# Attention's q and k parts stored once, stacks loaded in six transfers, expert weights loaded behind the attention rounds

## The chip, the cores and the metric

The kernel runs on one core of a Trainium2 chip. The core has a matrix engine (PE, with its weight loads shown apart as PEld), a vector engine (DVE), a scalar engine (ACT), a general engine (POOL) and a sync engine (SP), which here only issues transfers; 16 DMA engines move the data. The metric is the device time of one launch in microseconds (us), lower is better.

## The reference

Two transformer blocks with adaptive layer norm run one after the other on 16 sequences of 256 tokens and 128 features. The change lies in the attention of block 0:

```python
qkv = x @ w_qkv + b_qkv                     # 16 heads of depth 8
q, k = _rope(q), _rope(k)
scores = jnp.einsum('bhtd,bhsd->bhts', q, k) / jnp.sqrt(jnp.float32(D))
attn = jax.nn.softmax(scores, axis=-1)
out = jnp.einsum('bhts,bhsd->bhtd', attn, v)
out = jnp.transpose(out, (0, 2, 1, 3)).reshape(Bs, Ts, C) @ w_fc + b_fc
```

Behind it come a mixture of 64 experts (8 of them chosen for each token, and a shared one), the delta-rule attention of block 1, and its mixture of 8 experts.

## The kernel before, in words

Attention works in rounds, numbered n in the program and k in its Python: round n runs the projections of batch n + 2, the stack loads of batch n + 1, the first pass of scores of batch n (p1), the second pass of scores with exp and the product with v of batch n - 1 (p2), and the tail of batch n - 2. Each engine has its own instruction list, and semaphores order them; `run` calls `iteration` for rounds -3 to 17.

float32 scores are made from bfloat16: ACT cuts q and k into three parts each (`cut`, L439), all pairs of parts are stacked on 72 partitions (3 x 3 pairs x depth 8), and one matmul of 72 rows gives the score. To get the parts onto these partitions they go through DRAM. SP waits for the third cut and stores `at_part` into `qk_parts` (the tensor `bounce`), which holds all nine pairs of each batch: three stores for q (L592) and three for k (L594), each of all three parts, 192 KB. In the next round it loads the q stack (`at_qs`) and the k stack (`at_ks`) with one transfer of 72 rows of 8 KB each (L569). The q load waits for PE's first score of the round (`p1_done`) and for the stores (`part_out`); the k load waits for `nrows_in[1]`, that is for the last maxima rows of the batch before. PE waits for both (`stacked`) ahead of p1 of the next batch.

p1 (L191) gives the row maxima on DVE (L334), these are split into three parts, turned by PE (L175), copied by ACT to `at_npart`, and POOL moves them in two halves of the heads: a store to DRAM (L524, `max_parts<-at_npart`), a wait until it has landed, and a load into three more rows of the q stack (L529, `at_qs<-max_parts`). p2 (L204) waits for that load (`nrows_in[half]`): for half 0 ahead of head 0, for half 1 ahead of head 8.

The gate and up weights of the experts (`w_gu`) come in 16 pieces of 363 KB (L564). SP issues two of them at the end of each of the rounds 0 to 3 and 13 to 16, as `PIECE_ROUNDS` says; in rounds 14 to 16 SP has nothing else left but one k load. After the rounds it issues four small loads (L602), waits for the routing weights of the first chunk (`r0_kept`), stores them (L604), waits for that store and loads them spread over partitions (L609, nine transfers). Then all engines meet at the end of the block, and the experts' block starts, whose PE and ACT wait for all of `ffn0_loaded`: the 16 pieces and the four small loads.

Of the kernel before, what the change touches and what calls it, by code (L numbers as in the profile page):

```python
# [14 lines left out]
BF16 = mybir.dt.bfloat16  # L15
# [7 lines left out]
BATCH, SEQ = 16, 256  # L23
TOK = BATCH * SEQ
TILES = TOK // P
HEADS, DEPTH = 16, 8
# [9 lines left out]
PARTS = 3  # L36
PAIRS = PARTS * PARTS
ROWS = PAIRS * DEPTH
# [4 lines left out]
BUFS = 3  # L43
PEELED = 4
FIRST = -3
STACK_DMAS = 2
OUT_DMAS = 2 * PARTS
VW = 32
PIECE_ROUNDS = (0, 1, 2, 3, 13, 14, 15, 16)


def attention(nc, T, A, x_fm, x_tm, mod):
# [11 lines left out]
    with ExitStack() as ctx:  # L64
        def sb(name, shape, dt=F32):
            return ctx.enter_context(nc.sbuf_tensor(name, shape, dt))

        def sem(name):
            return ctx.enter_context(nc.semaphore(name))
# [6 lines left out]
        part = sb("at_part", [P, PARTS, 2 * SEQ], BF16)  # L76
# [21 lines left out]
        r0_bufs = (r0_sfc[:], r0_w[:], r0_hi[:], r0_lo[:], r0_th[:], r0_tl[:], r0_gs[:], r0_picked[:], r0_sig[:], r0_top[:],  # L98
                   r0_den[:], r0_rden[:])
        r0_ln = LayerNorm(nc, ctx, "r0_ln", T, r0_xc, T["h_fm"][:, 0:CHUNK], r0_nt, 0, 1)  # L100
        bounce = nc.dram_tensor("qk_parts", [BUFS, 2, PARTS, PARTS, DEPTH, HEADS, SEQ], BF16, kind="Internal").ap()
        nbounce = nc.dram_tensor("max_parts", [BUFS, 2, PARTS, HALF, SEQ], BF16, kind="Internal").ap()
        ps = T["psum"]
        P1, P2, OB, M0, M1 = [0, 1], [2, 3], (4, 5), 6, 7
# [17 lines left out]
        part_out = sem("at_part_out")  # L122
        stacked = sem("at_stacked")
# [6 lines left out]
        nrows_in = [sem(f"at_nrows_in{i}") for i in range(2)]  # L130
# [19 lines left out]
        def live(k):  # L150
            return {
                "xn": 0 <= k + 3 < BATCH, "proj": 0 <= k + 2 < BATCH, "load": 0 <= k + 1 < BATCH, "p1": 0 <= k < BATCH,
                "p2": 0 <= k - 1 < BATCH, "tail": 0 <= k - 2 < BATCH,
            }
# [5 lines left out]
        def run(eng, iteration):  # L160
            for n in range(FIRST, PEELED):
                iteration(n, n)
            with eng.Fori(0, (BATCH - 3 - PEELED) // BUFS) as i:
                for k in range(PEELED, PEELED + BUFS):
                    iteration(BUFS * i + k, k)
            for n in range(BATCH - 3, BATCH + 2):
                iteration(n, n)

        @block.tensor
        def _(pe):  # L170
# [8 lines left out]
            def scores(n, k, g, part=None):  # L179

                f = live(k)
                for h in heads(g, part):
                    if f["p1"]:
                        if h == 0:

                            pe.wait_ge(stacked, 16 * STACK_DMAS * (n + 1))
                        if k > 0 or h >= 2:
# [232 lines left out]
        def _(act):  # L420
# [10 lines left out]
            def cut(n, k, i):  # L431

                if i == 0:
                    act.wait_ge(qk_ready, n + 3)
                    if k >= -1:
                        act.wait_ge(part_out, 16 * OUT_DMAS * (n + 2))
                else:
# [112 lines left out]
        @block.sync  # L550
        def _(sp):
            def held(name, x):

                if isinstance(x, int):
                    return x
                r = sp.alloc_register(name)
                sp.reg_mov(r, x)
                return sp.snap(r)

            def load_weights(piece):  # L560

                start, name = (WG, "wg") if piece < WEIGHT_PIECES else (WU, "wu")
                at, size = piece % WEIGHT_PIECES, HIDDEN_ALL // WEIGHT_PIECES
                sp.dma_start(T["w_gu"][:, start + at * size:start + (at + 1) * size], A[name][:, at * size:(at + 1) * size])\  # L564
                    .then_inc(T["ffn0_loaded"], 16)

            def load_stack(buf, stack, q):

                sp.dma_start(stack[0:ROWS, buf, :, :], bounce[buf, q].rearrange("b a d h t -> (b a d) h t")).then_inc(stacked, 16)  # L569

            def iteration(n, k):
                f = live(k)
                cut = held(f"cut_{k}", PARTS * (n + 3))
                seen = held(f"seen_{k}", HEADS * n + 1)
                out = held(f"out_{k}", 16 * OUT_DMAS * (n + 2))
                rows_in = held(f"rows_in_{k}", 16 * n)
                if f["load"]:
                    if f["p1"]:

                        sp.wait_ge(p1_done, seen)  # L580
                    sp.wait_ge(part_out, out)
                    load_stack((k + 1) % BUFS, qs, 0)
                    if f["p2"]:

                        sp.wait_ge(nrows_in[1], rows_in)
                    load_stack((k + 1) % BUFS, ks, 1)
                if f["proj"]:

                    sp.wait_ge(part_ready, cut)
                    buf = (k + 2) % BUFS  # L590
                    for i in range(PARTS):
                        sp.dma_start(bounce[buf, 0, i].rearrange("a d h t -> (d h) a t"), part[:, :, 0:SEQ]).then_inc(part_out, 16)  # L592
                    for i in range(PARTS):
                        sp.dma_start(bounce[buf, 1, :, i].rearrange("b d h t -> (d h) b t"), part[:, :, SEQ:2 * SEQ])\  # L594
                            .then_inc(part_out, 16)
                if k in PIECE_ROUNDS:
                    for i in range(2):
                        load_weights(2 * PIECE_ROUNDS.index(k) + i)

            run(sp, iteration)  # L600
            for name in EARLY_LOADS:
                sp.dma_start(T[name][:], A[name]).then_inc(T["ffn0_loaded"], 16)  # L602
            sp.wait_ge(r0_kept, 1)
            sp.dma_start(T["rw_dram"][:, 0:CHUNK], r0_fm).then_inc(r0_out, 16)  # L604
            sp.wait_ge(r0_out, 16)
            rb = T["rw"][:, 1, :].bitcast(F32).rearrange("p (s c) -> p s c", c=CHUNK)
            for j in range(RB_SLOTS):
                for first, last, e in owners(j):
                    sp.dma_start(rb[first:last, j, :], T["rw_dram"][e:e + 1, 0:CHUNK].broadcast_to([last - first, CHUNK]))\  # L609
                        .then_inc(T["rb_in"][j], 16)  # L610
# [355 lines left out]
WEIGHT_PIECES = 8  # L966
# [24 lines left out]
def owners(j):  # L991

    rows = range(P * j, P * (j + 1))
    return [(max(HIDDEN * e, rows[0]) - rows[0], min(HIDDEN * (e + 1), rows[-1] + 1) - rows[0], e)
            for e in range(rows[0] // HIDDEN, rows[-1] // HIDDEN + 1)]
# [1038 lines left out]
def adaln_two_blocks(nc, *args):  # L2034
    A, out = dict(zip(NAMES, args[:-1])), args[-1]
    with ExitStack() as ctx:
# [23 lines left out]
        with ExitStack() as first:  # L2060
            for name, shape in dict(mean=[P, TILES], rstd=[P, TILES], w_qk=[P, 2 * D], w_v=[P, D], w_fc=[P, D],
                                    at_v=[P, BUFS, 2, HEADS, VW]).items():
                sb(name, shape, scope=first)
            sb("at_ks", [P, BUFS, HEADS, SEQ], BF16, scope=first)
            T["rw_dram"] = nc.dram_tensor("rw_fm", [EXPERTS, TOK], F32, kind="Internal").ap()
            setup(nc, T, A)
            attention(nc, T, A, T["x_fm"], T["x_tm"],
                      (T["scale1"][:, 0, :], T["shift"][:, 0, :], T["gate"][:, 0, :], T["ga_bfc"][:, :]))
# [62 lines left out]
```

## Time and profile before

| | us |
|---|---|
| median of 3 runs (lowest, highest) | 1827.18 (1826.78, 1829.08) |
| profiled execution, its own time | 1828.58 |
| span of the profile, first to last instruction | 1826.5 |

Times in the rows are us from the span's start. The attention rounds lie between about 20 and 377, the experts' block begins at 391.6. A timeline row has the start, the time taken, engine, line, operation, tiles, shapes and count, and in brackets how long the engine had been idle and what ended that. A windows row has the busy time of each engine in the stretch with its count of instructions, then the granted TensorE clock as a share of full speed, the mean busy share of the 16 DMA engines and what they moved.

### The profile page before, as it was taken

The page shows a single profiled execution, that of the slowest core. Times are in us where ns is not written, and L with a number is a line of the kernel's source. Part 1 is how long each engine was busy: PE and PEld are TensorE (multiplying, and loading weights), DVE is VectorE, ACT ScalarE, POOL GpSimd, SP SyncE. Part 2 cuts the span into 40 slices and gives each one's busy share as a digit, 9 for nine tenths or more (in the row PEclk, how much of TensorE's full clock was granted, in tenths as well). Part 3 has the DMA queues.
Part 4 walks back from the last instruction along what each step waited for, and adds up shares of the span by engine and source line. Part 5 has one row for each costly group of instructions (what it writes and reads, how often), then busy time and mean ns, then how long its engine had stood idle before and what let it go on. Part 6 is the DMA issues. An engine that isn't in the chain of part 4 may idle for free.

```text
span 1826.5 us, 25499 instructions
## 1 busy us (share of the span) xinstructions
PE 1659.0 (91%) x7212; PEld 1027.0 (56%) x7212; DVE 1366.2 (75%) x2636; ACT 819.6 (45%) x1533; POOL 691.8 (38%) x628
## 2 busy tenths in 40 slices
PE   3888888869989999999999999999998899899999
PEld 2455555446655656556665565655655555555555
DVE  4777777656979988979969889799698587544444
ACT  1566767657644234243352342533525543433333
POOL 2011111100002945928739469187394475000000
PEclk9989989989999999999999999999999999999999
DMA  6554445246575877677767666666671111111110
GB/s 199 152 157 129 119 111 152 89 125 215 180 207 188 222 205 204 210 209 214 215 189 203 187 188 197 189 197 204 190 194 52 41 47 52 35 57 53 52 52 23
DMA packets 172698, 269.49 MB, mean 148 GB/s; under 512 B 23748, under 2 KB 61981, under 8 KB 170053
## 3 DMA queue, kind: packets, MB, share of 16 engines
q1 hardware_dynamic: 168691, 266.33, 49.9%
q10 hardware_dynamic: 1874, 1.36, 0.2%
q0 software_dynamic: 2048, 0.79, 0.2%
q8 instruction: 37, 0.61, 0.1%
q14 instruction: 48, 0.39, 0.1%
HBM read 233.78 MB, written 34.62 MB: 147 GB/s over the span
## 4 chain that ended last, share of the span: by engine, by line
PE 36%; DVE 16%; issue 10%; POOL 10%; ACT 3%; DMA 3%; SPq 1%; DVEq 0%; POOLq 0%; ACTq 0%
PE psum L1528 10%; PE psum L1368 6%; POOL e_prod L1986 6%; PE psum L1370 6%; PE psum L1369 6%; PE psum L1383 5%; DVE psum L1897 4%; POOL e_phi L1986 3%; DVE e_hm L1900 2%; DVE e_vbar L1755 2%; DVE e_y L1755 1%; DVE e_state L1850 1%; DMA e_ring<-w_split 1%; PE psum L1462 1%; DMA rw<-rw_fm 1%
## 5 line engine op out<-in xcount | busy, mean ns | idle before, releaser
L1694 ACT ACTIVATE e_gu<-psum 128x512 f32<-128x512 f32 (+1 forms) x368 | 219.3, 598 | 545.5 <-PE psum L1370 284.3
L1368 PE MATMUL psum<-e_hhi,e_ring 128*128 128x512 f32 x704 | 434.0, 616 | 19.7 <-DMA e_ring<-w_split 11.5
L1383 PE MATMUL psum<-e_hm,w_d 128*128 128x512 f32 (+1 forms) x736 | 382.6, 601 | 15.0 <-DVE e_hm L1903 7.2
L1986 POOL TENSOR_TENSOR e_prod<-e_state,e_phi 128x512 f32<-128x512 f32 x256 | 353.4, 1417 | 2.4 <-POOL e_phi L1986 1.7
L1897 DVE TENSOR_TENSOR psum<-psum,rw 128x512 f32<-128x512 f32 x352 | 243.4, 692 | 90.9 <-PE psum L1370 85.1
L1935 DVE TENSOR_TENSOR e_hm<-psum,rw 128x512 f32<-128x512 f32 x256 | 174.6, 688 | 178.0 <-ACT psum L1722 176.9
L1369 PE MATMUL psum<-e_hhi,e_ring 128*128 128x512 f32 x704 | 279.0, 396 | 0.0
L1370 PE MATMUL psum<-e_hlo,e_ring 128*128 128x512 f32 x704 | 278.8, 396 | 0.0
L1900 DVE TENSOR_TENSOR e_hm<-psum,e_gu 128x512 f32<-128x512 f32 x352 | 243.5, 692 | 39.4 <-ACT e_gu L1694 15.7
L1528 PE MATMUL psum<-e_hm,w_gu 128*128 128x512 f32 x512 | 262.9, 598 | 6.6 <-DVE w_d L1916 5.5
L1722 ACT ACTIVATE psum<-psum 128x512 f32<-128x512 f32 x256 | 148.8, 582 | 254.7 <-PE psum L1370 238.8
L334 DVE TENSOR_REDUCE at_negm<-psum 128x2 f32<-128x512 f32 x256 | 163.0, 684 | 68.7 <-PE psum L191 67.8
L1368 PEld LDWEIGHTS psum<-e_hhi,e_ring 128*128 128x128 f32 x704 | 133.2, 189 | 139.7 <-issue 92.4
L1369 PEld LDWEIGHTS psum<-e_hhi,e_ring 128*128 128x128 f32 x704 | 133.4, 190 | 95.6 <-issue 82.6
L1383 PEld LDWEIGHTS psum<-e_hm,w_d 128*128 128x128 f32 (+1 forms) x736 | 136.0, 189 | 65.2 <-DVE e_hm L1900 18.7
L1986 POOL TENSOR_TENSOR e_prod<-e_vbar,e_phi 128x512 f32<-128x512 f32 x128 | 169.7, 1357 | 2.5
L1368 PE MATMUL psum<-e_hhi,w_gu_r 128*128 128x512 f32 x208 | 156.4, 752 | 10.1 <-DVE e_hlo L1741 8.1
L428 ACT ACTIVATE at_p<-psum 128x512 f32<-128x512 f32 x256 | 142.1, 590 | 26.2 <-PE psum L204 23.7
L1370 PEld LDWEIGHTS psum<-e_hlo,e_ring 128*128 128x128 f32 x704 | 132.6, 188 | 31.6
L1986 POOL TENSOR_TENSOR e_phi<-e_prod 128x480 f32<-128x480 f32 x32 | 30.6, 988 | 273.2 <-ACT e_beta L1653 273.2
L204 PE MATMUL psum<-at_qs,at_ks 75*128 75x256 bf16 x512 | 105.2, 290 | 14.2 <-DMA at_qs<-max_parts 12.3
L191 PE MATMUL psum<-at_ks,at_qs 72*128 72x256 bf16 x512 | 110.3, 302 | 8.2 <-DVE at_negm L334 3.5
(304 smaller groups left out, 2181.0 us busy)
## 6 DMA issues: line engine op xcount, KB each, us to landing
e_ring<-w_split SPq DMA_DIRECT2D x308, 256.0 KB, 4.2
rw<-rw_fm SPq DMA_DIRECT2D x192, 176.0 KB
qk_parts<-at_part SPq DMA_DIRECT2D x96, 192.0 KB, 3.1
rw<-gates_fm SPq DMA_DIRECT2D x72, 256.0 KB, 3.2
w_split<-e_ring SPq DMA_DIRECT2D x44, 256.0 KB, 2.7
rw<-rw_fm SPq DMA_DIRECT2D x64, 160.0 KB
at_qs<-qk_parts SPq DMA_DIRECT2D x16, 576.0 KB
at_ks<-qk_parts SPq DMA_DIRECT2D x16, 576.0 KB
```

The lines of the kernel that those rows point to most:

```text
L334: nc.vector.tensor_reduce(negm[:, k % BUFS, h // HALF, h % HALF, :], ps[:, P1[h % 2], :].rearrange("p (t s) -> p t s", t=2), AX.X, ALU.max ...
L1368: pe.matmul(out, w_hi, x_hi, start=first, stop=False)
L1369: pe.matmul(out, w_lo, x_hi, start=False, stop=False)
L1370: return pe.matmul(out, w_hi, x_lo, start=False, stop=last)
L1383: mm = pe.matmul(ps[:, ACC, :], weights_at(T, WD + P * j, P)[0:rows(j), :], hm[0:rows(j), slot(j), :], start=(j == 0), stop=(j == HT - 1))
L1528: pe.matmul(ps[:, ACC, :], weights_at(T, w2_low(j), P), hm[:, j % RING1, :], start=(j == 0), stop=(j == T1 - 1))\
L1694: a(act_g[0:r, j % 2, :], ps[0:r, GB[j % 2], :], ACT.Silu).then_inc(silu_done, 1)
L1722: a(ps[:, GU1[j % 2], :], ps[:, HB[j % 2], :], ACT.Gelu).then_inc(gelu_done, 1)
L1897: v.tensor_tensor(ps[:, bank(j), :], ps[:, bank(j), :], rb[:, s, :], ALU.mult).then_inc(gu_done, 1)
L1900: v.tensor_tensor(hm[:, slot(j), :], ps[:, bank(j), :], act_g[:, j % 2, :], ALU.mult).then_inc(hm_done, 1)
L1935: v.tensor_tensor(hm[:, j % RING1, :], ps[:, GU1[j % 2], :], rb[:, e % RB_SLOTS, :], ALU.mult).then_inc(m_done, 1)
L1986: ins = tt(out[:, at], x[:, at], y[:, at], op)
```

## The change

Each part is stored once: `qk_parts` has one copy of the three parts for q and one for k, and SP stores them with two transfers instead of six. The stacks are built by the loads: three transfers of 24 rows for q, each of all three parts, and three for k, each of which repeats one part three times by a source with step 0. The expert weights leave the rounds: behind the last round SP waits for both halves of the last maxima rows, and then issues all 16 pieces, ahead of the four small loads.

```diff
-STACK_DMAS = 2
-OUT_DMAS = 2 * PARTS
+STACK_DMAS = 2 * PARTS
+OUT_DMAS = 2
 VW = 32
-PIECE_ROUNDS = (0, 1, 2, 3, 13, 14, 15, 16)
...
-        bounce = nc.dram_tensor("qk_parts", [BUFS, 2, PARTS, PARTS, DEPTH, HEADS, SEQ], BF16, kind="Internal").ap()
+        bounce = nc.dram_tensor("qk_parts", [BUFS, 2, PARTS, DEPTH, HEADS, SEQ], BF16, kind="Internal").ap()
...
             def load_stack(buf, stack, q):
 
-                sp.dma_start(stack[0:ROWS, buf, :, :], bounce[buf, q].rearrange("b a d h t -> (b a d) h t")).then_inc(stacked, 16)
+                for b in range(PARTS):
+                    if q == 0:
+                        src = bounce[buf, 0].rearrange("a d h t -> (a d) h t")
+                    else:
+                        src = bounce[buf, 1, b].unsqueeze(0).broadcast_to([PARTS, DEPTH, HEADS, SEQ])
+                    sp.dma_start(stack[b * PARTS * DEPTH:(b + 1) * PARTS * DEPTH, buf, :, :], src).then_inc(stacked, 16)
...
-                    for i in range(PARTS):
-                        sp.dma_start(bounce[buf, 0, i].rearrange("a d h t -> (d h) a t"), part[:, :, 0:SEQ]).then_inc(part_out, 16)
-                    for i in range(PARTS):
-                        sp.dma_start(bounce[buf, 1, :, i].rearrange("b d h t -> (d h) b t"), part[:, :, SEQ:2 * SEQ])\
+                    for q in range(2):
+                        sp.dma_start(bounce[buf, q].rearrange("a d h t -> (d h) a t"), part[:, :, q * SEQ:(q + 1) * SEQ])\
                             .then_inc(part_out, 16)
-                if k in PIECE_ROUNDS:
-                    for i in range(2):
-                        load_weights(2 * PIECE_ROUNDS.index(k) + i)
 
             run(sp, iteration)
+            for half in range(2):
+                sp.wait_ge(nrows_in[half], 16 * BATCH)
+            for piece in range(WEIGHT_PIECES):
+                load_weights(piece)
+                load_weights(WEIGHT_PIECES + piece)
             for name in EARLY_LOADS:
                 sp.dma_start(T[name][:], A[name]).then_inc(T["ffn0_loaded"], 16)
             sp.wait_ge(r0_kept, 1)
```

## Rows read from the trace of the kernel before

**Rows 1.** Windows view: three attention rounds, then the slow-clock stretch of the third.

```profile
core 0: us, PE busy (x) PEld busy (x) DVE busy (x) ACT busy (x) POOL busy (x), PEclk, DMA share, GB/s
143.90:162.50 18.60, 16.34 (x156) 10.36 (x155) 15.26 (x35) 13.55 (x27) 2.79 (x5) 1.00 0.46 132
181.30:202.00 20.70, 17.99 (x156) 10.83 (x155) 15.72 (x35) 13.41 (x27) 2.86 (x5) 0.92 0.43 117
339.40:361.40 22.00, 17.11 (x146) 10.59 (x147) 11.73 (x26) 11.49 (x21) 3.79 (x7) 0.84 0.11 35
...
341.70:348.50 6.80, 5.27 (x33) 3.49 (x34) 1.04 (x2) 2.67 (x5) 0.53 (x1) 0.50 0.03 6
```

**Rows 2.** Waits of PE from 42 to 376: us in total, times, longest.

```profile
PE psum L204 <- DMA at_qs<-max_parts: 12.3, 6, 4.9
...
PE psum L191 <- DMA at_ks<-qk_parts: 1.9, 1, 1.9
```

**Rows 3.** Timeline of PE at the two longest of these waits.

```profile
62.68 0.61 PE L204 MATMUL psum<-at_qs,at_ks 75*128 75x256 bf16 x2 [4.85 <-DMA at_qs<-max_parts]
...
337.94 0.38 PE L191 MATMUL psum<-at_ks,at_qs 72*128 72x256 bf16 x2
343.23 0.61 PE L204 MATMUL psum<-at_qs,at_ks 75*128 75x256 bf16 x2 [4.90 <-DMA at_qs<-max_parts]
```

**Rows 4.** Timelines of POOL and SP ahead of them, and one undisturbed move (150.85).

```profile
53.02 0.71 POOL L524 DMA_DIRECT2D max_parts<-at_npart  x1 [38.81 <-ACT at_npart L487]
...
54.95 1.53 SPq L564 DMA_DIRECT2D w_gu<-in_wg  x2
...
56.62 0.51 POOL L529 DMA_DIRECT2D at_qs<-max_parts  x1 [2.90 <-DMA max_parts<-at_npart]
...
150.85 0.50 POOL L529 DMA_DIRECT2D at_qs<-max_parts  x1 [1.70 <-DMA max_parts<-at_npart]
...
330.44 0.32 SPq L569 DMA_DIRECT2D at_ks<-qk_parts  x1
330.80 3.70 SPq L564 DMA_DIRECT2D w_gu<-in_wu  x6
...
339.34 0.50 POOL L529 DMA_DIRECT2D at_qs<-max_parts  x1 [6.01 <-DMA max_parts<-at_npart]
```

**Rows 5.** Timelines of SP and PE: first stores, first stack loads, first scores.

```profile
28.61 1.49 SPq L592 DMA_DIRECT2D qk_parts<-at_part  x3
...
34.15 0.38 SPq L569 DMA_DIRECT2D at_qs<-qk_parts  x1
...
42.09 1.04 PE L191 MATMUL psum<-at_ks,at_qs 72*128 72x256 bf16 x4 [1.88 <-DMA at_ks<-qk_parts]
```

**Rows 6.** Windows view: a k stack load by itself, then weight pieces by themselves.

```profile
153.80:155.90 2.10, 0.92 (x8) 0.49 (x7) 2.07 (x5) 1.60 (x3) 0.00 (x0) 1.00 0.80 199
...
336.00:339.00 3.00, 2.33 (x24) 1.09 (x22) 2.61 (x8) 1.67 (x3) 0.00 (x0) 1.00 1.04 401
```

**Rows 7.** Timelines of SP, POOL and PE in one middle round.

```profile
152.90 0.30 SPq L569 DMA_DIRECT2D at_ks<-qk_parts  x1
154.96 1.48 SPq L592 DMA_DIRECT2D qk_parts<-at_part  x3
...
161.33 0.50 POOL L529 DMA_DIRECT2D at_qs<-max_parts  x1 [3.47 <-DMA max_parts<-at_npart]
...
162.78 0.38 PE L191 MATMUL psum<-at_ks,at_qs 72*128 72x256 bf16 x2
163.95 0.39 PE L204 MATMUL psum<-at_qs,at_ks 75*128 75x256 bf16 x2 [0.79 <-DMA at_qs<-max_parts]
```

**Rows 8.** Timelines of PE and SP from the last maxima rows to the block's end.

```profile
368.99 0.61 PE L204 MATMUL psum<-at_qs,at_ks 75*128 75x256 bf16 x4
...
385.28 0.51 SPq L604 DMA_DIRECT2D rw_fm<-r_xc  x1
387.62 3.44 SPq L609 DMA_DIRECT2D rw<-rw_fm  x9
```

## The prediction, made before the changed kernel ran

> **What bounds the kernel now.** The page comes first: the profiled execution took 1828.58 us with a span of 1826.5, and the diff touches only the part up to 391 us, so nothing behind the experts' start is worked on here; that part shifts as a whole. Then the windows view round by round, to see what a round costs and whether the DMA engines are its limit. They are not: a round takes 18.6 us at full clock and 20.7 when part of it runs at the lower clock, PE is busy for 16 to 18 of these and DVE for 15, while the DMA engines are less than half busy [rows 1]. So traffic that is removed gives time only where PE waits for a transfer, and the waits of PE are the next view. Over the attention stage PE waits 12.3 us for the maxima rows and 1.9 us for a stack [rows 2]; the rest of its gaps end with DVE or ACT. The timeline then shows where: two waits, of 4.85 and 4.90 us, are 9.75 of the 12.3, one in round 1 and one in round 15 [rows 3]. In both POOL's small moves were under way together with weight pieces. A move that lands undisturbed releases POOL 1.7 us after its issue, but the two moves of those places took 2.90 and then some 6 us (56.62 to PE's start at 62.68), and 6.01 and then 3.9 us [rows 3, 4]. SP had issued two pieces at 54.95 and six from 330.80 on. That is what the change can win; all else must be looked at for what it costs.
>
> **The stores.** Six stores of 192 KB become two. Three take SP 1.49 us to issue [rows 5], so issue falls from 3 us to 1 us a round. In the middle rounds nobody waits for them directly: SP's next q load waits for PE's first score, later than they land. Their traffic does delay POOL's half 0 move: 3.47 us instead of 1.70, with the stores issued from 154.96 on and the second move issued at 161.33 [rows 4, 7]. PE paid for that with 0.79 us at 163.95 [rows 7]; all such waits together are 12.3 - 9.75 = 2.5 us, of which I count at most 1.5 in the twelve middle rounds. Before the first round the stores are on the path: issued from 28.61 on, and SP starts the loads at 34.15 [rows 5]. Two fewer us of issue and a third of the bytes make that about 2.5 us earlier, 31.6.
>
> **The stack loads.** The bytes stay the same, 0.59 MB for each stack. Two transfers become six; at the 0.30 us that one load takes to issue [rows 7] SP spends some 1.3 us more a round, in stretches in which it waits anyway. The open price is the k load. Its three transfers read a source whose outermost count is 3, with step 0, which no large transfer of the trace has. Fast end: it runs as the load of 72 rows does, which by itself moved 199 GB/s with a DMA share of 0.80 [rows 6]; with about 0.9 us from issue to the first byte (152.90 to 153.80) and 0.5 at the end that lands in 4.5 us. Slow end: the three copies go to three of the sixteen engines. The weight pieces move 401 GB/s with all of them busy, 25 GB/s for each [rows 6]; three then give 75 GB/s, 7.9 us for 0.59 MB, and 9.3 us from issue to landing. I take the slow end: the same rows show that the spread follows a transfer's shape (128 rows keep all engines busy, 72 rows only 0.80 of them), and the shape has 3 outermost now.
>
> The Trainium skill, page "DMA: Bandwidth & Descriptors", section "Why a DMA increments its semaphore by 16 and not by 1", says that a transfer uses the largest number up to 16 which divides the outermost counts of both its sides. By that rule 72 rows would take 12 engines, 0.75 of them, and the trace has 0.80; 24 rows against 3 copies would take 3. Its section "Rules for kernel authors" warns of just this form, a leading broadcast of few copies. No row here shows three engines at work.
>
> What does 9.3 us hit? In the middle rounds the time from the k load's issue to PE's next first scores is 9.9 us in a round at full clock (152.90 to 162.78, [rows 7]), and some 2 us more in the longer rounds [rows 1], about half of the twelve; so the load just makes it, and each us beyond 9.9 costs a us in the six short ones, beyond 12 in all. The two new stores come behind the load on its three engines and land at about 11 us after its issue, when SP and ACT are just about to ask for them. POOL's half 0 move also falls into this time: it loses the stores' traffic and gets the k load's, on three engines only. Together I take +0.6 us for the middle rounds, between -1.5 (the waits above gone) and +6 (half a us in each).
>
> **Start.** At the slow end the loads start at 31.6, the q stack takes some 4 us and the k stack 7.9 us on the engines that both use, and first scores come at about 43.6 instead of 42.09 [rows 5]: 1.5 us late. POOL's first move, at 53.02, shifts by that to 54.5; without weights the two moves take about 2.5 us (1.7 and the issue itself) and 2.6 (161.33 to 163.95 is a second move without weights up to PE's start, [rows 4, 7]), so p2 starts at 59.6 instead of 62.68: a gain of 3.0 us, and not the full 4.85.
>
> **Round 15.** The k load of the last batch is issued at 330.44 and PE's scores start at 337.94, 7.5 us later [rows 3, 4]. At 9.3 us these scores start at 339.7, 1.8 us late, and p2 follows at about 340.7, if POOL's moves have landed by then (its first one was issued by 333.3, 6.01 us ahead of 339.34; an answer after 1.7 us and 2.6 from there give 337.6, and up to 3 more beside the k load). Against 343.23 that is a gain of 2.5 us. Behind the old wait the clock was 0.50 for 6.8 us [rows 1], where a middle round with a share of 0.92 over 20.7 us has about 3.3. Half speed over the 3.5 us in excess costs at most 1.7 us; I take half of it, 0.8.
>
> **The weights at the end.** SP wakes when the last rows land, at 368.99, where PE starts its p2 on them [rows 8]. 16 pieces are 5.9 MB, 14.8 us at 401 GB/s [rows 6]; six pieces took 3.70 us to issue [rows 4], so issue (9.9 us) is hidden by the data. With 0.9 us ahead of the first byte and some 1.5 us for the four small loads all is in at about 386.2. The store of the routing weights is issued at 385.28 and was answered 2.34 us later, at 387.62 [rows 8]; its data now queues behind the last pieces, a loss of 0.5 us. What hides the rest is attention's tail and the routing from 369 to 385, which uses no transfer. The slowest rate of the rows, the stack load's 199 GB/s [rows 6], is the other bound: 6.2 MB would then take 31 us and end at 401, a loss of 15 us. The rate of the same transfers is the nearer row.
>
> **Sum.** -3.0 (start) - 2.5 (round 15) - 0.8 (clock) + 0.6 (middle rounds) + 0.5 (end) = -5.2 us. From 1828.58 that is 1823.4 for the profiled execution. It stands 1.4 us above the median of the runs; from 1827.18 the forecast is 1822.0.
>
> **Rivals.** *The k load is as wide as before.* Then it lands in 4.5 us, first scores come at about 39, and POOL's moves put p2 at 54.7: a gain of 8.0 us. Round 15 gains the whole 4.9, the clock 0.8 and the middle rounds 1.5, less 0.5 at the end: -14.7, 1812.5. For it: the bytes and the 8 KB rows are those of the load that ran at 199 GB/s. Against it: the outer count of 3. Chance 0.22.
>
> *The weights at the end eat the gain.* At 290 GB/s the 6.2 MB end at 391.3, the loss is 5.5 us and the sum about 0: 1827. At 330 GB/s the time would be 1825, at 245 GB/s 1831, and at the bound of 199 GB/s 1836. For it: all is in one queue, and the routing store stands behind it. Against it: the 401 GB/s were measured on the same transfers, and nothing else runs. Chance 0.15.
>
> *The k load is late in every round.* If three engines move less than 75 GB/s, or POOL's rows and the stores stretch their queue, it lands 12 us after its issue, say: PE then waits 2.1 us in the six short rounds and 2.7 us more than forecast in round 15, 15 us less the 0.6 of the sum, so 1836. At 13 us all twelve rounds wait and it is 1850. The sign turns at about 10.7 us of landing, 64 GB/s. For it: the load has no margin in the short rounds. Against it: three engines have fewer rivals for memory and ports than twelve. Chance 0.17.
>
> **How the numbers follow.** The forecast has 0.46. A measurement of this kernel tells about 0.2%, 3.7 us, from no change. The forecast itself lies between 1815 and 1828 (the start from -8 to -1, middle rounds from -1.5 to +6), 0.40 of it faster and 0.06 the same. With the wide load's 0.22, faster has 0.62; the late weights give 0.12 to the same and 0.03 to slower; the late k load gives 0.16 to slower and 0.01 to the same: 0.19 and 0.19. The range is 1811 to 1835: it takes in the wide load, most of the late weights and the mildest late k loads, and leaves out the rest of these.
>
> **What would show it.** Right: PE's waits for the maxima rows in rounds 1 and 15 fall below 1 us; the windows around a k load show a DMA share near 0.2 and some 75 GB/s; PE waits for `at_ks` in round 15 and a little in tight middle rounds; the routing store is answered within 3 us of its issue. Wrong: a k load at 0.7 to 0.8 share (the wide rival); PE waiting for `at_ks` in every round; the block's end more than 2 us later after the last maxima rows than the 18.6 us from 368.99 to 387.62; or the clock, if the rounds' lower stretches change in number, which I can't forecast and which are worth some 1.7 us each.

## The result, and the profile after

The changed kernel takes 1836.91 us (median of 7 runs, 1833.38 to 1846.11) against 1827.18 (7 runs, 1820.63 to 1832.50): the ratio, which goes by all runs and not by the medians, is 1.0065, with a 95% interval of 1.0037 to 1.0093. It is slower, by 7 to 17 us, where 1822.0 was forecast. Its profiled execution took 1833.38 us with a span of 1831.4, which is the fastest of its runs. The accounting below therefore covers 4.9 us of the difference, less than the lower end of that interval.

PE's timeline after, at the places of [rows 3, 5 and 8] and at the start of round 14's first scores (328.77; before it was 320.92):

```profile
43.49 1.03 PE L190 MATMUL psum<-at_ks,at_qs 72*128 72x256 bf16 x4 [5.38 <-DMA at_ks<-qk_parts]
...
62.75 0.61 PE L203 MATMUL psum<-at_qs,at_ks 75*128 75x256 bf16 x2 [3.94 <-DMA at_qs<-max_parts]
...
328.77 0.38 PE L190 MATMUL psum<-at_ks,at_qs 72*128 72x256 bf16 x2
...
349.09 0.39 PE L203 MATMUL psum<-at_qs,at_ks 75*128 75x256 bf16 x2
...
372.79 0.61 PE L203 MATMUL psum<-at_qs,at_ks 75*128 75x256 bf16 x4
```

SP's timeline after, with the first stores and loads, a middle round, and the end:

```profile
28.62 0.92 SPq L596 DMA_DIRECT2D qk_parts<-at_part  x2
31.41 1.13 SPq L573 DMA_DIRECT2D at_qs<-qk_parts  x3
32.59 2.33 SPq L573 DMA_DIRECT2D at_ks<-qk_parts  x3
...
153.64 2.19 SPq L573 DMA_DIRECT2D at_ks<-qk_parts  x3
155.87 0.96 SPq L596 DMA_DIRECT2D qk_parts<-at_part  x2
...
372.13 0.37 SPq L563 DMA_DIRECT2D w_gu<-in_wg  x1
...
389.08 0.53 SPq L608 DMA_DIRECT2D rw_fm<-r_xc  x1
392.77 3.44 SPq L613 DMA_DIRECT2D rw<-rw_fm  x9
396.79 0.36 SPq L1315 DMA_DIRECT2D w_d<-in_wd  x1
```

With the same points of before these rows give the time stage by stage (the first `w_d` load of the experts was issued at 391.64 before):

| up to | before | after | of this stage | forecast |
|---|---|---|---|---|
| p2 of batch 0 | 62.68 | 62.75 | +0.07 | -3.0 |
| first scores of batch 14 | 320.92 | 328.77 | +7.78 | +0.6 |
| p2 of batch 14 | 343.23 | 349.09 | -1.99 | -2.5 |
| p2 on the last rows | 368.99 | 372.79 | -2.06 | -0.8 |
| routing store issued | 385.28 | 389.08 | 0.00 | 0 |
| routing loads issued | 387.62 | 392.77 | +1.35 | +0.5 |
| first `w_d` load of the experts | 391.64 | 396.79 | 0.00 | 0 |

The sum is +5.15, and 0.25 comes back in the experts. So the end of the attention stage went nearly as forecast, and the loss lies in the start, which gained nothing, and in the middle rounds. POOL's timeline after shows what happens at both places (the first move of batch 0, half 0 and half 1 of a middle round, then half 0 of batch 14):

```profile
53.99 0.71 POOL L523 DMA_DIRECT2D max_parts<-at_npart  x1 [39.78 <-ACT at_npart L486]
58.73 0.51 POOL L528 DMA_DIRECT2D at_qs<-max_parts  x1 [4.03 <-DMA max_parts<-at_npart]
...
151.63 0.50 POOL L528 DMA_DIRECT2D at_qs<-max_parts  x1 [2.10 <-DMA max_parts<-at_npart]
157.81 0.54 POOL L523 DMA_DIRECT2D max_parts<-at_npart  x1 [5.67 <-ACT at_npart L486]
164.40 0.51 POOL L528 DMA_DIRECT2D at_qs<-max_parts  x1 [6.05 <-DMA max_parts<-at_npart]
...
341.60 0.54 POOL L523 DMA_DIRECT2D max_parts<-at_npart  x1 [4.54 <-ACT at_npart L486]
346.65 0.50 POOL L528 DMA_DIRECT2D at_qs<-max_parts  x1 [4.51 <-DMA max_parts<-at_npart]
```

A move is two transfers, a store and a load; the number in brackets at the load is the time that POOL was idle until the store was answered. The half 0 move of the same batch was answered after 3.47 us before [rows 7]; now it takes 6.05, and over the twelve middle rounds (batches 2 to 13) 4.45 to 6.05, against 2.6 to 4.35 before. The half 1 move, whose load goes out 6 us before half 0's store, is nearly as quick as it was (1.65 to 2.3 us, but 4.3 for batch 13, where it was 3.4). What is in flight beside half 0 is the k load of 153.64, with the stores of 155.87 behind it. The windows of that stretch, of a round, and of the routing store after:

```profile
core 0: us, PE busy (x) PEld busy (x) DVE busy (x) ACT busy (x) POOL busy (x), PEclk, DMA share, GB/s
124.22:144.66 20.44, 17.99 (x155) 10.87 (x154) 15.82 (x36) 13.44 (x26) 2.78 (x5) 0.92 0.28 80
...
160.00:163.00 3.00, 3.00 (x17) 1.86 (x19) 2.51 (x4) 1.99 (x4) 0.00 (x0) 0.50 0.20 64
...
389.00:393.00 4.00, 0.00 (x0) 0.00 (x0) 0.00 (x0) 0.06 (x1) 0.00 (x0) 0.50 0.46 126
```

From 160 to 163 only the tail of the k load and POOL's small packets are under way: a share of 0.20 and 64 GB/s, where a k load by itself had 0.80 and 199 [rows 6]. A whole round moves 80 GB/s instead of some 120 to 130 [rows 1], and is no shorter. PE's waits for transfers over the attention stage after:

```profile
PE psum L203 <- DMA at_qs<-max_parts: 11.3, 10, 3.9
...
PE psum L190 <- DMA at_ks<-qk_parts: 7.0, 2, 5.4
```

Before, the wait for the rows was 12.3 us in 6 times, nearly all in two places [rows 2]; now it is 11.3 in 10 times. From 80 to 320 us it rose from 1.5 to 5.9 us. The two waits for the k stack are at 43.49 (5.38) and at 82.05 (1.63).

Waits are not the whole of the middle rounds. Their windows, from p2 of batch 0 to the first scores of batch 14, before and then after:

```profile
core 0: us, PE busy (x) PEld busy (x) DVE busy (x) ACT busy (x) POOL busy (x), PEclk, DMA share, GB/s
62.68:320.92 258.24, 231.50 (x1966) 140.28 (x1967) 195.64 (x432) 172.75 (x332) 34.99 (x63) 0.93 0.47 131
...
62.75:328.77 266.02, 235.74 (x1967) 141.05 (x1968) 196.19 (x433) 173.60 (x332) 35.05 (x63) 0.90 0.27 78
```

For the same matmuls PE is busy 4.2 us longer, at a granted clock of 0.90 instead of 0.93. These are means; single stretches show 1.00 or 0.50, and the mean says how much of each there was.

### The profile page after: what moved, and what is told of

Same layout as the page of the kernel before. It is cut to its first block, busy times and chain, and to the rows that moved or that the text cites. A ratio compares the mean times of both kernels' runs of the same rounds, so it can differ in the third digit from the quotient of the medians.

```text
span 1831.4 us, 25497 instructions
## 1 busy us (share of the span) xinstructions
PE 1664.1 (91%) x7212; PEld 1027.3 (56%) x7212; DVE 1366.3 (75%) x2636; ACT 820.4 (45%) x1533; POOL 692.0 (38%) x628
## 4 chain that ended last, share of the span: by engine, by line
PE 32%; DVE 20%; issue 11%; POOL 7%; DMA 3%; ACT 3%; SPq 1%; DVEq 1%; POOLq 0%; ACTq 0%
PE psum L1532 10%; PE psum L1372 5%; PE psum L1374 5%; PE psum L1373 5%; DVE psum L1901 5%; POOL e_prod L1990 4%; PE psum L1387 4%; POOL e_phi L1990 3%; DVE e_hm L1904 3%; DMA e_ring<-w_split 2%; DVE e_vbar L1759 2%; DVE e_state L1854 2%; DVE e_y L1759 2%; PE psum L1466 1%; DVE e_hm L1939 1%
## 5 line engine op out<-in xcount | busy, mean ns | idle before, releaser
L203 PE MATMUL psum<-at_qs,at_ks 75*128 75x256 bf16 x512 | 106.4, 293 | 13.3 <-DMA at_qs<-max_parts 11.3
```

## The experiments

Each ratio is against runs of before on the same chip; "waits" are PE's for the maxima rows and for the k stack up to 420 us. Theory N: what costs is POOL's half 0 move, answered only behind the narrow k load. Rivals: W, the weights at the end; T, the number of transfers; later L, PE's own k stack lands late; B, bytes alone.

**e1_weights_only.** Before, with the weight pieces moved behind the rounds and nothing else:

```diff
-PIECE_ROUNDS = (0, 1, 2, 3, 13, 14, 15, 16)
...
             run(sp, iteration)
+            for half in range(2):
+                sp.wait_ge(nrows_in[half], 16 * BATCH)
+            for piece in range(WEIGHT_PIECES):
+                load_weights(piece)
+                load_weights(WEIGHT_PIECES + piece)
```

> Only the weights move behind the rounds; stores and stacks stay as before. Theory N (the narrow k load on three engines is what costs, through POOL's half 0 move): the two long waits of PE go, -8 to -10 us, the end gives back 1.4, the rounds in the middle stay; about 1819, 6 to 9 us below before. Theory W (the weights at the end are what costs): 2 us or more above before, as in the changed kernel.

1819.13 us, ratio 0.9933 (0.9908 to 0.9958), waits 4.2 and 1.8 us; the routing store was answered after 3.97 us (370.79 to 374.76). Moving the weights is a gain of some 12 us in spite of the store; W falls.

**e2_stacks_only.** The changed kernel with the weight pieces back in their rounds.

```diff
+PIECE_ROUNDS = (0, 1, 2, 3, 13, 14, 15, 16)
```

> Only the stores and stack loads change; the weights stay in their rounds. Theory N: as slow as the changed kernel or slower, 1836 to 1846, POOL's half 0 move answered some 6 us after its issue in the middle rounds. Theory W: no slower than before, 1822 to 1828.

1859.3 us, ratio 1.0155 (1.0125 to 1.0184). PE's waits:

```profile
PE psum L204 <- DMA at_qs<-max_parts: 30.3, 15, 6.1
...
PE psum L191 <- DMA at_ks<-qk_parts: 17.2, 6, 6.1
```

So the new stores and loads are the loss, and a larger one than I expected: with the pieces in the rounds too, PE waits 30.3 us for the rows and 17.2 for the k stack itself. Added up, e1's -0.67% and e2's +1.55% make +0.9%, which the intervals just allow beside the measured +0.65%.

**e3_depth_outer.** The changed kernel with the rows of both stacks in another order, so that the k load's source has 8 outermost and not 3 (the q load's 8 and not 24); the count of transfers and the bytes stay.

```diff
-                        src = bounce[buf, 0].rearrange("a d h t -> (a d) h t")
+                        src = bounce[buf, 0].rearrange("a d h t -> d a h t")
...
-                        src = bounce[buf, 1, b].unsqueeze(0).broadcast_to([PARTS, DEPTH, HEADS, SEQ])
+                        src = bounce[buf, 1, b].unsqueeze(1).broadcast_to([DEPTH, PARTS, HEADS, SEQ])
```

> The changed kernel with the rows of each stack in another order, depth outside and part inside, so that each transfer's source has 8 outermost instead of 3 (k) or 24 (q); same bytes, same six loads and two stores, same products. Theory N: the k load moves 170 GB/s or more and lands in 5 us, POOL's half 0 move is answered in 2.0 to 2.6 us, PE waits under 2 us in all for the maxima rows, 1811 to 1818. Theory T (six loads instead of two are what costs, by their number on SP and in the queues): no faster than the changed kernel, 1834 to 1840.

1819.87 us, ratio 0.9936 (0.991 to 0.9961), waits 9.3 us (13 times, longest 2.0) and 3.3. The shape of the transfers alone is worth some 1.3%, and T falls. But N had the way wrong here. The waits did not go below 2 us as expected: from 80 to 320 us PE waits 8.7 us for the rows, more than the 5.9 of the changed kernel. Half 0 moves of the middle rounds were answered in 2.2 to 5.1 us, and half 1 moves were slower than there (3.00 and 3.19 us at 147.13 and 166.91), perhaps beside the q load, which has 8 outermost now too; that was not tried. What e3 gains lies mostly in the start, where p2 of batch 0 begins at 56.53 instead of 62.75, and in the middle rounds, 258.9 us instead of 266.0, where PE is busy 230.4 us instead of 235.7 at a clock of 0.95 instead of 0.90.

**e4_k_as_before.** The changed kernel with k stored three times and loaded by one transfer of 72 rows, as before; q keeps its one store and three loads.

```diff
+        kbounce = nc.dram_tensor("k_parts", [BUFS, PARTS, PARTS, DEPTH, HEADS, SEQ], BF16, kind="Internal").ap()
...
+                if q == 1:
+                    sp.dma_start(stack[0:ROWS, buf, :, :], kbounce[buf].rearrange("b a d h t -> (b a d) h t")).then_inc(stacked, 16)
+                    return
...
+                    for i in range(PARTS):
+                        sp.dma_start(kbounce[buf, :, i].rearrange("b d h t -> (d h) b t"), part[:, :, SEQ:2 * SEQ])\
+                            .then_inc(part_out, 16)
```

> The changed kernel with the k side as before: parts of k stored three times, one load of 72 rows; the q side stays changed (one store, three loads of 24 rows). Theory N: the narrow load is gone, POOL's half 0 move is answered in 2.5 to 3.3 us beside four stores, 1813 to 1821. Theory T: four loads instead of six leave half of the loss, 1830 to 1834.

1815.64 us, ratio 0.9929 (0.9902 to 0.9957): faster than both kernels. PE's waits:

```profile
PE psum L204 <- DMA at_qs<-max_parts: 3.3, 4, 1.5
...
PE psum L191 <- DMA at_ks<-k_parts: 2.6, 1, 2.6
```

The k side alone is the loss, and with e3 its load's form. From 80 to 320 us PE waits 1.2 us for the rows, and the half 0 moves are answered after 2.9 us in the mean, against 4.9 in the changed kernel. Against e1 the q side brings nothing that these intervals can tell.

**e5_spare_narrow and e6_spare_wide.** These leave e4's k load as it is and add idle traffic behind it, 590 KB a round that no instruction reads, in the narrow form or in the wide one. Only SP waits for it, a round later and once behind the rounds.

```diff
                     load_stack((k + 1) % BUFS, ks, 1)
+                    if k >= 0:
+                        sp.wait_ge(r0_out, spare_in)
+                    buf = (k + 1) % BUFS
+                    spare = [ks[96:120, 0, :, :], ks[96:120, 1, :, :], qs[96:120, 0, :, :]]
+                    for b in range(PARTS):
+                        src = bounce[buf, 0, b].unsqueeze(0).broadcast_to([PARTS, DEPTH, HEADS, SEQ])  # e5
+                        src = bounce[buf, 0].rearrange("a d h t -> (a d) h t")  # e6
+                        sp.dma_start(spare[b], src).then_inc(r0_out, 16)
```

> This is e4 (k stored three times and loaded by one transfer of 72 rows, q changed, weights behind the rounds; 1815.6 us) with 590 KB a round of idle traffic behind the k load: three transfers of one q part repeated three times, 24 rows each, in the same form as the changed kernel's k load, into rows of the stacks' tiles that no instruction reads, so that neither the matmuls nor the k load depend on them. Theory N (the narrow load costs because POOL's move of the half 0 maxima is answered only behind it): the move's answer goes from about 2 to 5 us and more in every round, TensorE waits 9 to 14 us in all for the move, and the time is 1830 to 1840 us, most of the way back to the changed kernel's 1837. Rival L (the narrow load costs because TensorE's own k stack lands late, and the move is a bystander): the k load is as wide and early as in e4, so 1814 to 1822 us, waits as in e4 (3.3 and 2.6 us).

> e4 with the same 590 KB of idle traffic a round at the same place, but as three transfers of 24 different rows, in the form of the q loads. Theory N: the traffic is spread over more engines, each holds the move for 2 us at most, TensorE waits 4 to 7 us in all for the move, 1815 to 1823 us. Rival B (bytes cost, whatever engines carry them: stores, loads and moves share the memory): the same as e5, within 3 us.

e5 took 1880.6 us, ratio 1.0284 (1.0258 to 1.0311); e6 1849.84 us, ratio 1.0124 (1.009 to 1.0158). Against e4's ratio that is 3.6% and 2.0%. PE's waits, of e5:

```profile
PE psum L204 <- DMA at_qs<-max_parts: 46.6, 14, 5.1
...
PE psum L191 <- DMA at_ks<-k_parts: 2.7, 1, 2.7
```

and of e6:

```profile
PE psum L204 <- DMA at_qs<-max_parts: 30.1, 15, 5.4
...
PE psum L191 <- DMA at_ks<-k_parts: 3.0, 1, 3.0
```

L falls as the only cause: PE's k stack is as early as in e4, 2.7 us of waits, and the time is lost all the same, in the wait for the moves. But both sizes are far outside what N expected, and the answer to the move's store does not tell e5 from e6: in the middle rounds it took 4.65 to 5.2 us in e5 and 4.5 to 6.9 in e6. Traffic on more engines holds it too, if there is this much of it. What differs is the move's second transfer. From its load to PE's start on the rows, one round of e5 and then one of e6:

```profile
181.47 0.51 POOL L529 DMA_DIRECT2D at_qs<-max_parts  x1 [4.78 <-DMA max_parts<-at_npart]
186.24 0.61 PE L204 MATMUL psum<-at_qs,at_ks 75*128 75x256 bf16 x2 [2.79 <-DMA at_qs<-max_parts]
...
173.81 0.50 POOL L529 DMA_DIRECT2D at_qs<-max_parts  x1 [6.11 <-DMA max_parts<-at_npart]
175.89 0.39 PE L204 MATMUL psum<-at_qs,at_ks 75*128 75x256 bf16 x2 [1.45 <-DMA at_qs<-max_parts]
```

That is 3.1 to 4.8 us in the middle rounds of e5 in which PE waited, and 2.0 to 2.2 in e6 from batch 3 on. The other half of the difference is PE's clock: over the middle rounds e5 took 301.8 us and e6 272.9, and of these 28.9 us PE was busy for 14.6, at a granted clock of 0.86 instead of 0.91. So form and bytes both count, and in the same bytes the narrow form cost nearly twice as much, where both transfers of the move were held and PE spent longer at the lower clock. N holds for the way in which the narrow load reaches the move; it was too narrow in its condition and left out the clock.

**e7_store_by_act and e8_half_earlier.** Two tries at the end of e4: the routing store on ScalarE's own queue, and half of the weight pieces ahead of the last half 1 move.

```diff
+            act.wait_ge(r0_kept, 1)
+            nc.scalar.dma_start(T["rw_dram"][:, 0:CHUNK], r0_fm).then_inc(r0_out, 16)
```

```diff
             for half in range(2):
                 sp.wait_ge(nrows_in[half], 16 * BATCH)
-            for piece in range(WEIGHT_PIECES):
-                load_weights(piece)
-                load_weights(WEIGHT_PIECES + piece)
+                for piece in range(WEIGHT_PIECES // 2 * half, WEIGHT_PIECES // 2 * (half + 1)):
+                    load_weights(piece)
+                    load_weights(WEIGHT_PIECES + piece)
```

> e4 with one change at the end: the routing weights' first store is issued by ScalarE on its own queue and not by SyncE behind the 16 weight pieces. If the 1.3 us that the routing store took more in the changed kernel comes from its place behind the weight pieces in SyncE's queue, its answer comes within 2.5 us (it took 3.7 to 4.0) and the time falls by 1 to 1.6 us against e4: 1814 us. If it comes from the 410 GB/s that the pieces still move, the answer takes 3.5 to 4 us and the time is e4's, 1815.6 us.

> e4 with the first eight of the 16 weight pieces issued already behind the last half 0 move and before the half 1 move, some 8 us earlier. The routing store then meets the tail of the small loads only and is answered within 2.5 to 3 us (gain 0.7 to 1.5 us); the last half 1 move shares the engines with eight pieces of data and lands 1 to 5 us later, of which the cover in front of it hides some. Sum: 1813 to 1820 us, no more than 0.2% from e4.

e7: 1820.95 us, ratio 0.9956 (0.9936 to 0.9976); e8: 1822.17 us, ratio 0.9965 (0.9943 to 0.9987). Neither beats e4. In e7 the store still took 3.98 us (372.10 to 376.08), so it is not its place in SP's queue. The windows of e7 show the last of the weights still moving up to it, and beside it:

```profile
368.00:372.00 4.00, 1.73 (x8) 0.86 (x8) 2.53 (x14) 1.56 (x3) 0.73 (x1) 1.00 1.03 406
372.00:376.00 4.00, 0.00 (x0) 0.00 (x0) 0.00 (x0) 0.07 (x1) 0.00 (x0) 0.66 0.54 163
```

In e8, where the weights had landed, it took 2.33 us (381.51 to 383.84), as before; but the last half 1 move went out 24.7 us behind the last batch's first scores (336.29 to 360.96) instead of 21.1 in e4 (334.73 to 355.86), which costs more.

**e9_k_spread and e10_k_early.** The changed kernel with two of the three k transfers, or all of them, issued right behind the q loads, ahead of SP's wait for the half 1 rows.

```diff
+                    load_stack((k + 1) % BUFS, ks, 1, range(2))             # e10: all three
                     if f["p2"]:
 
                         sp.wait_ge(nrows_in[1], rows_in)
-                    load_stack((k + 1) % BUFS, ks, 1)
+                    load_stack((k + 1) % BUFS, ks, 1, range(2, PARTS))      # e10: none
```

> The changed kernel with the same nine transfers a round in the same forms, only issued elsewhere: two of the three k transfers go out right behind the q loads (in the profile after 146.2 us instead of 153.6), the third stays where all three stood. Theory N says that what costs is the small move that falls into the narrow load: two transfers are done some 6 us after issue, before the half 0 move of 157.8 us; the third needs 3 us and is done at 157. Half 0 is answered in 1.5 to 3 us again (6.05 in the changed kernel), the half 1 move (149.0 and 151.6) meets the tail of the early pair and takes some 1 to 2 us more, and the time comes to 1816 to 1826 us. Rival B (the bytes and the narrow form cost wherever they stand): no more than 3 us from the changed kernel's 1837.

> The same, with all three k transfers right behind the q loads, 7.5 us earlier than in the changed kernel: the narrow load then covers 146 to 156 us, where the half 1 move stands and not the half 0 move. Theory N: half 0 is answered in 1.5 to 3 us, half 1 in 4 to 6 us (2.1 in the changed kernel), TensorE's wait for at_qs moves to heads 8 and up, and the k stack is never waited for; 1820 to 1840 us by how much cover half 1 has. Rival L (the k stack's late landing): the waits for the k stack go from 7.0 us to at most 2.6 and with them the time, to 1825 to 1831, whichever move stands in the load.

e9 took 1862.14 us, ratio 1.0186 (1.016 to 1.0212), with waits of 35.6 and 6.3 us; e10 took 1899.81 us, ratio 1.039 (1.0362 to 1.0418), with 58.0 and 5.8. POOL's timeline in a middle round of e10, half 0, half 1 and half 0 again:

```profile
184.99 0.50 POOL L528 DMA_DIRECT2D at_qs<-max_parts  x1 [1.64 <-DMA max_parts<-at_npart]
...
201.97 0.50 POOL L528 DMA_DIRECT2D at_qs<-max_parts  x1 [4.96 <-DMA max_parts<-at_npart]
...
211.90 0.50 POOL L528 DMA_DIRECT2D at_qs<-max_parts  x1 [1.65 <-DMA max_parts<-at_npart]
```

This is the cleanest sign of the mechanism: the delay moved with the load. Half 0 fell to 1.64 us, its undisturbed time [rows 4], and half 1 rose from 2.10 to 4.96. The packet records of the traces say the same in more detail. Each store of a move ends in 16 packets of 4 bytes. In the middle rounds of the changed kernel 13 of half 0's 16 had ended 2.0 us after its issue, and the last three 4.0 to 5.7 us after it, in every one of the twelve rounds; half 1's were all early but for batch 13. In e10 it is half 1 that has three late ones, 4.2 us or more after its issue, in all twelve. In e9 both were held: in one round half 1 for 5.06 us and half 0 for 3.76, about as long as beside the stores before (3.47, [rows 7]).

The times I expected were wrong, and the rows give three reasons. PE's start behind the e10 move above:

```profile
196.48 0.53 POOL L523 DMA_DIRECT2D max_parts<-at_npart  x1 [3.07 <-ACT at_npart L459]
...
205.95 0.61 PE L203 MATMUL psum<-at_qs,at_ks 75*128 75x256 bf16 x2 [4.46 <-DMA at_qs<-max_parts]
```

First, less work covers half 1: PE is ready for it some 5 us after its store (205.95 less 4.46 is 201.49; 4.7 to 5.4 us in e9 and e10), and ready for half 0 only 6.0 to 7.4 us after its store in those rounds of the changed kernel, behind the start, in which it waited. In e9 the whole half 1 move, from store to PE's start, took 7.3 to 8.2 us, no longer than half 0 in the changed kernel (7.1 to 8.2), and it cost 2.2 to 3.1 us in each round with a wait, instead of 0.2 to 2.0. Second, in e10 the load was held as well, 4.0 us from 201.97 to 205.95 where 2.1 is usual. Third, PE was busy longer for the same matmuls: 265.8 us over the middle rounds of e10, at a granted clock of 0.81, and 247.2 in e9, at 0.86. Behind SP's wait for the half 1 rows the k load stands at the less bad of the two places.

## Why the prediction was wrong, point by point

**The k load's form: right.** Three engines, forecast at 75 GB/s and a share near 0.2; 64 GB/s and 0.20 were measured in the window of its tail. The Trainium skill's rule (page "DMA: Bandwidth & Descriptors", section "Why a DMA increments its semaphore by 16 and not by 1") gave three engines of sixteen, 0.19, and the trace agrees with 0.20. The landing was a little mis-sized: by the packet records the load's last packet ended 9.95 to 10.3 us after its issue in the middle rounds instead of 9.3. In the round of 153.64 the first packet started 1.5 us after the issue and not 0.9, and the 72 rows took 8.6 us and not 7.9.

**The step that failed: what 9.3 us of narrow load hit.** I looked at the reader of the stack, PE, and found that it would just make it; for the middle rounds that is nearly so, with one wait of 1.63 us. Of POOL's half 0 move I wrote that "it loses the stores' traffic and gets the k load's, on three engines only", and took +0.6 us for the middle rounds with +6 as the bound. They lost 7.8. Three of the 16 closing packets of the half 0 move's store came 4.0 to 5.7 us after its issue, when the other 13 had long ended: I read this as the three busy engines holding the last ones while the others idle. The answer then takes 4.45 to 6.05 us, with a share of 0.20 to 0.28 over all engines. Of the 7.8 us PE's waits show 6.0 (4.4 more for the rows, 1.6 for the stack). Beside them PE is busy 4.2 us longer at the lower granted clock and waits 2.5 us less for ACT; the clock the prediction had named and left out of its sum. That this part comes from the change is not shown: e4, e7 and e8 have the same middle rounds as one another, and their profiles have PE busy there for 231.1, 228.1 and 234.3 us and the rounds 257.5, 254.2 and 260.9 us long.

**Start: -3.0 forecast, +0.07.** The loads' issue (31.41, forecast 31.6), first scores (43.49, forecast 43.6) and POOL's first move (53.99, forecast 54.5) came as said. The step behind them failed: I gave the two transfers of the move 2.5 and 2.6 us "without weights", and they took 4.7 (53.99 to 58.73) and 4.0 (to 62.75). For the first the reason is the same: the next k load, issued at 45.74 and ended 10.7 us later by its packets, and the stores of 52.71 were under way. The second began when they were over. Beside it ran the next q load:

```profile
58.84 1.13 SPq L573 DMA_DIRECT2D at_qs<-qk_parts  x3
```

From 58 to 59 the DMA share was 0.00, and from 62 to 63 it was 1.00. The 2.6 us came from a round in which the q load went out only near the end of that transfer (163.19, for 161.33 to 163.95). In e4 and e3 the q load went out 1.5 and 2.5 us behind the move's load, and not 0.1, and PE started 2.95 and 2.2 us after that load. What the q load adds was not tried by itself.

**Round 15 and the stretch behind it: near in number, not in the way.** -2.0 and -2.1 against -2.5 and -0.8. I had PE wait for the k load and p2 follow. The k load of the last batch went out at 338.67 and its scores began at 348.74, without a wait, because PE was slower in front of them. The stretches from that k load to p2 of batch 14 and from there to p2 on the last rows, before and then after:

```profile
core 0: us, PE busy (x) PEld busy (x) DVE busy (x) ACT busy (x) POOL busy (x), PEclk, DMA share, GB/s
330.44:343.23 12.79, 7.56 (x70) 4.13 (x71) 7.08 (x16) 5.81 (x11) 2.32 (x4) 0.94 0.76 244
343.23:368.99 25.76, 23.52 (x212) 14.61 (x213) 15.34 (x41) 18.17 (x34) 5.17 (x9) 0.90 0.02 4
...
338.67:349.09 10.42, 10.39 (x71) 5.30 (x71) 5.79 (x13) 5.50 (x11) 1.04 (x2) 0.67 0.16 59
349.09:372.79 23.70, 21.27 (x214) 13.20 (x213) 15.85 (x42) 18.48 (x35) 6.44 (x11) 1.00 0.02 5
```

The wait of 4.90 us is gone, but 2.8 us of that went into matmuls at the lower clock, which now stands ahead of p2; behind p2 it is at 1.00, and that is the 2.1. The half 0 move was held here too, 4.51 us, and the slower PE covered it. That the sum came near is partly luck.

**Weights at the end: right within its bounds.** +1.35 instead of +0.5, as the store shares the engines with the last pieces (e7, e8). What the move is worth elsewhere shows without the narrow load: some 12 us (e1), with 8.1 us less of waits for the rows, near the 9.75 of the two long waits [rows 3]. In the changed kernel the narrow load took all of that back and more.

**The rivals.** The late k load gave 1836 to 1850 us, and the time is there, but by another way: PE waits for the stack twice, not in every round. The three engines did move less than the 75 GB/s, as it said, though more for each (64 is 21 for each) than those that carried the k load before (199 GB/s at a share of 0.80 [rows 6] is 16); why is not shown. The wide load was the right counterfactual: with a wider k load (e1, e3, e4) the time is 1816 to 1820 us; 1812.5 was forecast.

## What to carry to other kernels

When a transfer is made longer, look not only at who reads its data, but at every small transfer that is in flight beside it, and at what waits for that one's answer; a share of 0.2 over all engines says nothing about the three that are full. Saving bytes was worth nothing here, where no one waited for them, and a broadcast source with few copies outermost paid for them in time. Look at the granted clock of a stage beside its waits, and don't put down a few us of one stage to a change from a single profile: the same middle rounds took 254.2 to 260.9 us. Change the two halves of an edit by themselves: here one half won 0.7% and the other lost 1.6%.

## What the runs showed of the hardware that was not expected

- A small move beside a transfer on three engines is answered in 4.45 to 6.05 us: 13 of its 16 closing packets have ended after 2.0 us, and three come at 4.0 to 5.7. Undisturbed it takes 1.64 to 1.70 us.
- Three loads with a step 0 source take SP 2.19 us to issue, three of the same size without it 1.13 us. Step 0 is not the reason: e3's q loads, of the same size and without it, took 2.08 us (159.61).
- 590 KB more a round in the wide form cost e6 2.0% against e4, at a DMA share of 0.50 from 80 to 320 us (e4: 0.39).
- With longer waits PE's granted clock was lower too: over the middle rounds, for the same 1966 matmuls, PE was busy 231.1 us at 0.92 in e4, 247.2 at 0.86 in e9 and 265.8 at 0.81 in e10, with 1.2, 26.4 and 34.9 us of waits for the rows from 80 to 320 us.
